# Causal masks as two triangles of 64 columns in a hybrid attention and FFN kernel, with a new order of the work

## The reference

```
x = x + attn_a(layernorm(x))     # 16 heads of 8, RoPE, causal over 256 tokens, softmax, Wo
x = x + ffn(layernorm(x))        # FP4 quantise-dequantise of x, w and h in blocks of 16; silu(gate) * up; down
x = x + attn_b(layernorm(x))     # 16 heads, causal within windows of 32 tokens, RMS norm on q and k
x = x + ffn(layernorm(x))        # the same weights again
```

## Time and profile before

| | |
|---|---|
| median of 3 runs | 422.82 us (422.71 to 425.64) |
| the profiled execution, its own time | 420.45 us |
| its span, first to last instruction | 418.6 us |
| PE matmul busy | 327.8 us (78%), 3533 instructions |
| DVE busy | 293.8 us (70%), 746 instructions |
| ACT busy | 242.2 us (58%), 630 instructions |
| POOL busy | 150.2 us (36%), 210 instructions |

### The profile page before, as it was taken

One profiled execution on the slowest core, in us unless ns is written; L12 is line 12 of the kernel. 1 busy time (PEld: TensorE's weight loads), 2 busy tenths in 40 slices (PEclk: granted clock), 3 DMA queues, 4 the chain that ended last, 5 costly groups with the idle time before them and its releaser, 6 DMA issues.

```text
span 418.6 us, 9181 instructions
## 1 busy us (share of the span) xinstructions
PE 327.8 (78%) x3533; PEld 220.8 (53%) x3533; DVE 293.8 (70%) x746; ACT 242.2 (58%) x630; POOL 150.2 (36%) x210
## 2 busy tenths in 40 slices
PE   1416689778989997999999989997898676665844
PEld 1314446445666754767676666665457445453523
DVE  2835323839677889699987989788747867847741
ACT  2300064226578485488689789787669475592421
POOL 6230042213362037181572251603822553523323
PEclk9999968869899989999999999999699799998565
DMA  6252026605125025020451000000000000000000
GB/s 176 80 113 37 4 76 118 134 3 128 26 81 89 5 63 89 4 78 2 79 128 27 2 4 2 3 16 14 2 2 14 2 0 14 2 14 1 13 14 13
DMA packets 33103, 17.49 MB, mean 42 GB/s; under 512 B 1874, under 2 KB 32914, under 8 KB 33060
## 3 DMA queue, kind: packets, MB, share of 16 engines
q1 hardware_dynamic: 32772, 16.78, 18.3%
q10 hardware_dynamic: 288, 0.13, 0.1%
HBM read 9.37 MB, written 7.34 MB: 40 GB/s over the span
## 4 chain that ended last, share of the span: by engine, by line
PE 39%; DVE 25%; ACT 15%; issue 12%; POOL 4%; DMA 3%; SPq 2%; DVEq 0%; POOLq 0%; ACTq 0%
DVE bmax L1360 6%; PE fb L881 5%; PE fb L799 4%; PE ffb L997 4%; PE fb L869 3%; PE fb L838 3%; ACT prob L1083 2%; PE ffb L975 2%; PE lb L938 2%; PE ffb L991 2%; PE fb L888 2%; PE fb L871 2%; ACT Kd L1126 1%; PE fb L840 1%; PE ffb L979 1%
## 5 line engine op out<-in xcount | busy, mean ns | idle before, releaser
L1360 DVE TENSOR_REDUCE bmax<-fb 128x3 f32<-128x384 f32 x128 | 66.8, 549 | 20.7 <-PE fb L841 19.7
L1083 ACT ACTIVATE prob<-fb 128x384 f32<-128x384 f32 x128 | 59.3, 496 | 24.0 <-PE fb L872 23.3
L838 PE MATMUL fb<-Kf,Qf 48*128 48x256 bf16 x128 | 32.2, 300 | 13.3 <-DMA Kf<-scr_f 7.3
L869 PE MATMUL fb<-Qf,Kf 51*128 51x256 bf16 x128 | 31.3, 295 | 5.2 <-ACT prob L1083 4.4
L840 PE MATMUL fb<-maskb 64*128 64x256 bf16 x128 | 32.3, 300 | 0.0
L1222 POOL TENSOR_TENSOR qk<-ra,rb 128x512 f32<-128x512 f32 x7 | 8.9, 1272 | 63.9 <-DVE rb L1341 63.9
L871 PE MATMUL fb<-maskb 64*128 64x256 bf16 x128 | 31.1, 292 | 0.0
L881 PE MATMUL fb<-prob,Vf 128*32 128x128 f32 (+1 forms) x512 | 29.9, 354 | 1.4 <-ACT prob L1083 1.2
L838 PEld LDWEIGHTS fb<-Kf,Qf 48*128 48x128 bf16 x128 | 10.6, 94 | 31.3 <-DVE bmax L1360 17.5
L839 PE MATMUL fb<-Kf,Qf 48*128 48x128 bf16 x128 | 25.5, 234 | 0.0
L841 PE MATMUL fb<-maskb 64*128 64x128 bf16 x128 | 25.3, 232 | 0.0
(11 more groups left out here) (201 smaller groups left out, 962.7 us busy)
## 6 DMA issues: line engine op xcount, KB each, us to landing
scr_f<-partsf SPq DMA_DIRECT2D x16, 192.0 KB, 2.3
Qf<-scr_f SPq DMA_DIRECT2D x16, 192.0 KB, 3.6
Kf<-scr_f SPq DMA_DIRECT2D x16, 192.0 KB, 5.0
scr_f<-partsf SPq DMA_DIRECT2D x16, 128.0 KB, 1.9
xall<-in_L_attn_a_x_dram SPq DMA_DIRECT2D x8, 128.0 KB, 4.9
scr_f<-partsf SPq DMA_DIRECT2D x16, 64.0 KB, 1.6
out_dram<-xall SPq DMA_DIRECT2D x8, 128.0 KB, 1.8
ropet<-in_rope_dram SPq DMA_DIRECT2D x1, 512.0 KB, 4.1
```

Of the source, the lines that this page charges most:

```text
L838: pe.matmul(S[:, 128:384], Qf[k, g, 128:256], Kf[k, g, 0:256], start=True, stop=True, skip_group_check=True)
L869: pe.matmul(S[:, 128:384], Kf[k, g, 0:128], Qf[k, g, 0:256], start=True, stop=True, skip_group_check=True)
L1083: act.activation(prob[:, slot % 8, :], S[:, 0:384], ACT.Exp).then_inc(f.s_exp, 1)
L1360: dve.tensor_reduce(bmax[:, h, 1:4], fb[:, h % 2, 0:384].rearrange("p (n k) -> p n k", k=P), AX.X, ALU.max).then_inc(bmax_done, 1)
```

## The change

The causal mask of a diagonal tile of 128 x 128 has four quarters of 64 x 64: a triangle, nothing, a triangle, and one wholly masked quarter (first half of the queries, second half of the keys). Before, the first mask matmul wrote a triangle and the constant quarter together, 128 columns for each tile. Now it writes the triangle only, 64 columns. The constant quarter comes out of the score matmuls: two more rows in the stacks, `Qf` one where the token is in quarter 0 (in the other row, quarter 2), `Kf` -1e30 where the token is in quarter 1 (quarter 3). `front2` score matmuls read 50 rows, `front3` ones 53. At the start six more DMAs load the rows of `Qf`, and the six of `Kf` carry five rows instead of three. The mask constants have 128 columns fewer.

The order of all engines is written anew, and so is `FFN_TURNS`. The words that came with the change also name maxima subtracted by DVE; the diff has no such edit, and `local2` does so before and after.

```diff
 NSTACK = HD * NC
-KROWS = NSTACK + 3
+MROWS = NSTACK + 2
+KROWS = MROWS + 3
...
-    full = np.full((64, 64), NEG)
-    halves = np.concatenate([eye[0:64], eye[64:128], lower, full, full, upper], 1)
+    halves = np.concatenate([eye[0:64], eye[64:128], lower, upper], 1)
+    tok = np.arange(SEQ)
+    q_rows = [tok // 64 == 0, tok // 64 == 2]
+    k_rows = [np.where(tok // 64 == 1, NEG, 0.0), np.where(tok // 64 == 3, NEG, 0.0)] + 3 * [np.ones(SEQ)]
...
-        "ones": bf16_bits(np.ones((3, PAIRS * SEQ))),
+        "ones": bf16_bits(np.tile(np.stack(q_rows + k_rows), (1, PAIRS))),
...
             for i in range(RING):
                 for r in range(2):
-                    sp.dma_start(Kfs[i][64 * r + NSTACK:64 * r + KROWS, :, :].rearrange("p g t -> p (g t)"), ones.bitcast(BF16)).then_inc(k_loaded, 16)
+                    sp.dma_start(Kfs[i][64 * r + NSTACK:64 * r + KROWS, :, :].rearrange("p g t -> p (g t)"), ones.bitcast(BF16)[2:7, :]).then_inc(k_loaded, 16)
+                    sp.dma_start(Qfs[i][64 * r + NSTACK:64 * r + MROWS, :, :].rearrange("p g t -> p (g t)"), ones.bitcast(BF16)[0:2, :]).then_inc(k_loaded, 16)
...
-                    row = 64 * r + NSTACK
+                    row = 64 * r + MROWS
...
-                            pe.wait_ge(k_loaded, 16 * (1 + 2 * RING))
+                            pe.wait_ge(k_loaded, 16 * (1 + 4 * RING))
...
-                    k = slice(64 * r, 64 * r + NSTACK)
+                    k = slice(64 * r, 64 * r + MROWS)
...
-                    pe.matmul(ends(S, 0, 128), eye_lo[half_, :], twice(m_qk[half_, :]), start=False, stop=True, skip_group_check=True)
-                    mm = pe.matmul(ends(S, 64, 64), eye_hi[half_, :], twice(m_qk[half_, 0:64]), start=False, stop=True, skip_group_check=True)
+                    pe.matmul(ends(S, 0, 64), eye_lo[half_, :], twice(m_qk[half_, :]), start=False, stop=True, skip_group_check=True)
+                    mm = pe.matmul(ends(S, 64, 64), eye_hi[half_, :], twice(m_qk[half_, :]), start=False, stop=True, skip_group_check=True)
...
-                        pe.matmul(two(S[:, 0:256], 0, 128), eye_hi[half_, :], twice(m_kq[half_, :]), start=False, stop=True, skip_group_check=True)
-                        mm = pe.matmul(two(S[:, 0:256], 0, 64), eye_lo[half_, :], twice(m_kq[half_, 64:128]), start=False, stop=True, skip_group_check=True)
+                        pe.matmul(two(S[:, 0:256], 64, 64), eye_hi[half_, :], twice(m_kq[half_, :]), start=False, stop=True, skip_group_check=True)
+                        mm = pe.matmul(two(S[:, 0:256], 0, 64), eye_lo[half_, :], twice(m_kq[half_, :]), start=False, stop=True, skip_group_check=True)
```

More of the change, by code:

```diff
@@ L63 @@
     "sp.front1": """
-0 1
-8 9
+5 9
 11 12
-15 16
+13 15
+16 17
 19 20
-22 23
-25 27
+23 24
+25 26
 28 29""",
     "sp.front2": """
-7
+10
 14
-17
+18
 21
-24
-26
+22
+27
 30
@@ new lines @@
+445 447 448 450 452 453 456 458 459 461 462 465 466 470 471 475 476 478 479 481 483 489 492""",
+    "pe.local1": """
+123 135 158
+191 196 212
+255 259 267
+321 324 334
+384 389 405
+455 457 468
+497 500 508
+530 531 534""",
+    "pe.local2": """
+163 167 171 175 181 184
+221 222 232 233 236 241
+272 277 294 296 304 305
+343 346 357 362 373 376
+414 420 431 432 439 443
+474 477 485 486 491 494
+512 513 518 519 521 524
+538 539 544 545 546 547""",
+    "pe.ffn_a2": """
+71 74 83 88 92
+128 139 144 149 153
@@ new lines @@
+199 203 204 209 211
+256 260 262 265 266
+316 320 323 325 328
+392 396 399 401 402
+460 463 464 467 469
+505 506 507 509 510""",
+    "pe.ffn_b2": """
+218 223 224 234 237
+271 285 289 299 306
+375 377 378 382 383
+442 446 449 451 454
+493 495 496 498 499
+511 514 515 516 517
+532 533 535 536 537
+552 553 554 555 556""",
+    "pe.ffn_a3": """
+114 116 117 118
+173 174 176 178
+239 240 242 244
+307 309 310 312
+364 365 367 370
+434 435 438 440
+484 487 488 490
+520 522 523 525""",
+    "pe.ffn_b3": """
@@ L181 @@
+333 338 339 350
+409 412 425 429
+472 473 480 482
+501 502 503 504
+526 527 528 529
+540 541 542 543
+548 549 550 551
 557 558 559 560""",
     "act.weights": """
[L183 removed]
+4 5""",
     "act.front1": """
[L185 to L192 removed]
+0 1 2 3
+7 10 13 16
+24 29 32 34
+39 48 49 53
+72 79 82 83
+107 116 117 123
+169 190 193 200
+214 224 225 228""",
     "act.front2": """
[L194 to L202 removed]
[7 rows of a table removed]
@@ new lines @@
+74 78 87 91 94 100
+121 125 130 136 137 141
+172 176 180 183 184 188
+219 223 227 231 233 237
+262 265 268 274 277 283
+314 317 322 329 330 334
+355 357 361 365 367 371
+386 387 388 390 392 394""",
+    "act.local2": """
+109 110 115
+146 151 158
+202 203 207
+243 247 257
+290 295 304
+341 346 352
+376 377 380
+396 399 401""",
+    "act.ffn_a1": """
+36 38
+71 73
+118 126
+163 170
+208 213
+260 264
+310 316
+356 360""",
+    "act.ffn_a2": """
+42 45 56
+86 89 96
+131 135 138
+177 181 187
+218 222 229
@@ L263 @@
+271 275 279
+325 328 333
+366 368 370""",
+    "act.ffn_b1": """
+129 134
+166 173
+212 215
+269 280
+313 321
+359 364
+382 385
+403 405""",
+    "act.ffn_b2": """
+143 147 156
+195 201 206
+258 259 263
+306 308 320
+353 354 358
+372 375 378
 391 393 395
-403 405 407""",
+407 408 409""",
     "act.ffn_a3": """
-54 67 68
-118 142 144
-149 175 176
-198 211 212
-237 252 253
-300 322 323
-337 345 346 351
-371 372 373 374""",
-    "act.ffn_b3": """
-179 196 197
-259 295 297
-307 341 343
-348 369 370
@@ L279 @@
-377 387 388
-394 400 401
-404 406 408 409
+65 68 70
+103 111 112
+145 159 160
+192 209 211
+240 253 254
+286 300 301
+337 338 348 349
+373 374 379 381""",
+    "act.ffn_b3": """
+162 235 241
+255 289 292
+303 342 345
+351 362 363
+369 383 384
+389 397 398
+400 402 404 406
 410 411 412 413""",
@@ L289 @@
 11 14 15 16
-17 22 23 26
-27 28 29 33
-34 39 41 44
-45 51 52 53""",
+17 23 24 25
+26 30 32 34
+35 47 49 51
+54 60 61 64""",
     "pool.local1": """
-20 24
-38 43
-48 58
-60 65
-67 72
-83 84
-90 94
-101 105""",
+21 27
+31 38
+43 48
+59 62
+68 73
+78 84
+89 95
+104 106""",
     "pool.ffn_a1": """
 12 13
-21 25
-30 31
-40 47
-56 59
-68 69
-77 82
-89 92""",
-    "pool.ffn_b1": """
-32 37
-57 61
-64 66
-73 74
-75 79
-93 95
-104 106
-109 110""",
+20 22
+33 36
+42 45
+55 58
+69 71
+79 82
+91 94""",
+    "pool.ffn_b1": """
@@ L321 @@
+37 39
+44 46
+57 66
+72 74
+80 83
+93 96
+103 105
+112 114""",
     "pool.ffn_a3": """
 18 19
-35 36
-42 46
-54 55
-62 63
-76 78
+28 29
+40 41
+50 53
+63 65
+75 76
 85 86 87 88
-97 98 99 100""",
+99 100 101 102""",
     "pool.ffn_b3": """
-49 50
-70 71
-80 81
-91 96
-102 103
+52 56
+67 70
+77 81
+90 92
+97 98
 107 108
-111 112 113 114
+109 110 111 113
 115 116 117 118""",
     "dve.weights": """
-3 4 5 6 9 10""",
+4 6 7 9 13 15""",
     "dve.front1": """
-0 1 2 7 8 11 12
-13 14 15 37
+0 1 2 3 5 8 10
```

260 lines of the change are left out of this document (82 added, 178 removed), and 110 rows, old and new, of tables (FFN_TURNS, TIMES).

## The result

| | before | changed |
|---|---|---|
| median of 4 runs, taken in turns | 422.76 us (418.78 to 425.64) | 408.02 us (406.49 to 410.12) |
| ratio, 95% interval | | 0.9685 (0.960 to 0.977) |
| profiled execution, its own time | 420.45 us | 406.49 us |
| its span | 418.6 us | 404.6 us |
| PE matmul busy | 327.8 us | 315.1 us |

The kernel became 3.2% faster, where 414.8 us (1.9%) was forecast. So ratios can differ by some tenths of a per cent from a quotient of medians. A second series of runs of the changed kernel gave 0.973 (0.970 to 0.976).

What follows compares the result with a forecast made beforehand. The prediction took PE, 91% busy in the middle, as the bound, DVE next. From a 418.6 us span, masks -6, start -2 and rest of the order 0 gave 410.6, or 414.8 us as median of runs; range 407.5 to 421.5.

Steps and rivals of the forecast that it cites:

- The masks, -6 us: Mask matmuls of front2 and front3, 128 columns fewer 256 times: 6 us less, nearer the chain's 5.5 than the ceiling.
- PE's queue is full there, and a matmul taken from it is time given back: Middle, 60 to 290 us: PE 91% busy, longest wait 3.9 us, so removed matmuls save time until DVE is next limit.
- The ceiling of 12 us: Middle: the most the shorter masks can give, 240 mask matmuls at 0.05 us of PE each.
- the share of L840 and L871 in the chain: First mask matmuls, 2% and 1% of the chain that ended last: 12.6 us, half of it removed, 6.3 us.
- the gain goes into the next limit: Rival, chance 0.15: DVE and ACT's exponentials set front2 and front3; the masks give 1.5 us, 419.3 us in all.
- The start, -2 us: Start's new order: RoPE ahead of FFN weights, head 2 1.2 us earlier, shorter front2(0) pairs 0.75 us; together 2 us.
- a gap ahead of the third: Sign at the start, in front2(0): a 2 us gap ahead of the third bmax, where PE's weights transposes stand.
- The rest of the order, 0 us: New order of middle and end: work moved ahead delays front3(7) and is missing in the end; taken as 0 us.
- The bound of -3: Lower bound on the new order of middle and end: at best 3 us less, with +4 as the other bound.
- whose 91 us hardly shrink, being one batch's latency: End, from batch 7's front residual to its last add: 91 us, held to be one batch's latency that hardly shrinks.
- The clock: Rival, chance 0.04: fewer columns get PE a lower granted clock in the middle; with 0.87 the time is 433 us.
- a last L1397 near 317 us: Sign: the last front residual's last row lies near 317 us, the end 91 us behind; beyond 322 us is wrong.

Runs made afterwards that it cites:

- order_only: The kernel before with its old masks and the changed kernel's new order on every engine; ratio 0.9715 to the kernel before.
- masks_only: The kernel before's order on every engine, with the new masks, stack rows and start DMAs; ratio 1.003 to the kernel before.
- start_and_masks: New masks, rows and DMAs, with the new order up to 60 us and the old order after; ratio 0.994 to the kernel before.
- start_only: Old masks and DMAs, with the new order up to 60 us and the old order after; ratio 0.986 to the kernel before.
- end_only: Old masks, with the old order up to 325 us and the new order from there; ratio 0.998 to the kernel before.
- rest_of_order: Old masks, with the old order up to 60 us and the new order for the rest; ratio 0.984 to the kernel before.
- no_triangles: The changed kernel with both triangle mask matmuls of each head left out in front2 and front3; ratio 0.972 to the kernel before.

## Why the prediction was right, and where it was not

The time lies in the range and on the side that had most of the chance. The sum came out at -8 us where the profiled span moved by -14 (by -11 in the repeat), and two of its three terms were mis-sized in opposite directions: the 6 us that it gives to the masks came from the order. That the total still lies in the range is luck, and the side was right because the start and the rest of the order were worth more than they were priced at.

*The masks, -6 us: measured 0 in the time of the whole kernel.* The difference between the change and order_only is within half a per cent of nothing (0.9685 and 0.973 against 0.9715; the intervals allow some 2 us either way), masks_only is at 1.003, and start_and_masks is no better than start_only. The step that failed is "PE's queue is full there, and a matmul taken from it is time given back". It rested on 91% of busy time and on 3.9 us of shown waits. The 3.9 us are the longest group only; all shown waits of PE there add up to 18 us. Both views are blind to pauses under 0.16 us, and columns stream in 74% of the stretch. The ceiling of 12 us was wrong too, since it counted matmuls one after the other of which many run side by side: 7 us by the table. The rest of the costing held: L846 and L847 start 0.06 us apart, the two more rows are free, DVE's maxima keep their length. The other support, the share of L840 and L871 in the chain, isn't a saving either. The chain passes through those matmuls, but it doesn't tell how soon another chain, by way of DVE or ACT, would have ended, and the runs say that one does so almost at once. Of the rivals, "the gain goes into the next limit" had this mechanism and still left the masks 1.5 us. In profiles the last front residual does start 3.5 to 5.5 us earlier with the new masks (322.6 in order_only, 319.1 and 317.2 in the change), near the 6 us, and the spans are 2.4 and 5.6 us shorter. The times of all runs don't bear that out. One place where such a gain can go is in the table of the experiments, and the prediction didn't ask about it: the length of the end goes with its granted clock. In the new order it is 86.9 to 87.6 us at 0.81 to 0.82, 88.7 at 0.79 and 90 at 0.77; in the old order 94 us at 0.80 to 0.81, 95.2 at 0.78 (end_only) and 96.4 to 96.7 at 0.77. All five executions with 0.77 have the new masks, but the two of the change, which has them too, had 0.82 and 0.79. Whether a shorter front brings the lower clock or it is chance is open.

*The start, -2 us: measured -2.5 to -6.* start_only has -6 (0.986), start_and_masks, which has the masks too, -2.5 (0.994). The links stood in the after trace nearly as forecast: remainder 0.69 us (0.7), first scores at 29.69 (30.5), first `bmax` 30.44 (31.4), a gap ahead of the third of 1.64 (2), pairs 1.36 us apart (1.37), and the six DMAs 1.9 us, hidden behind RoPE. The third part is ready at 20.4 us (21.0), SP reads 2.4 us later (2.1 + 0.6), and head 2 starts 2.66 us behind head 0 (3.0). Together head 2 starts 2.3 us earlier (34.67 to 32.35), not 1.2. Why 2.3 us there become up to 6 at the end is not shown.

*The rest of the order, 0 us: measured -7.* rest_of_order has 0.984. The bound of -3 was too near. What failed is "whose 91 us hardly shrink, being one batch's latency". From the last front residual to the last add they shrink to 84.9 us, and to the end of the span from 94.0 to 87.5, with old masks too (87.6 in order_only, 86.9 in rest_of_order). The end is not one batch's latency. Batch 7's steps share their queues with what batches 5 and 6 have left, and less is left when local and FFN work goes ahead in the middle. That batch 7's scales no longer wait for batch 6's adds isn't the gain by itself, for end_only has that too and gains nothing. The prediction named that effect and set it off against a delay of front3(7). The delay came in front3(6), by 4 us in order_only, and was made up by front3(7). That both the middle and the end of the new order are needed is shown (0.998 with the new end alone, 0.991 without it); how much each carries can't be told from these runs.

*The clock*, 0.04: in the changed kernel the middle has 0.94 against 0.95, nothing worth a term. The end, where its executions differ, was not in this rival.

The check "a last L1397 near 317 us" came true (317.15), as the sum's parts had it, and would have been read as proof of the masks' term. The repeat of the same kernel has 319.1. The other half of that check, the last add 91 us behind it, did not come true (84.9).

## What to carry to other kernels

Before pricing a matmul that is taken away, lay out its columns over the granted clock and see how much of the span they fill; if a quarter is unfilled, PE's busy share says little, and an engine with a lower share can be the one on the path. The quickest test is to leave out much more of the suspected work than the change does: twice the mask columns gave nothing, which settled in one experiment what shares and chains had got wrong. Before a small difference between two traces is explained, compare their granted clocks stage by stage. And split a change that rewrites an order from the edit that came with it, since here the order was the whole gain, part of it in a drain that looked like fixed latency.

## What the runs showed of the hardware that was not expected

A matmul's record in the trace is 0.16 us longer than its columns at full clock (0.22 for 0.055), whatever follows it. With some 2500 matmuls in 230 us this fills most gaps: 91% are shown as busy in the kernel before where 74% are streamed, and from it to no_triangles the view lost 12 us where streaming lost 20. The Trainium skill ("Perfetto Trace Analysis", the note at its head) says that matmul busy time is a bad metric for how close a kernel is to its roofline, the most that the engine can do, because matmuls are pipelined; the trace agrees.

Matmuls of 48 to 64 rows on different halves of the array ran side by side without being asked to, two of 256 columns in 0.12 us, which takes 18 of 79 us off the scores and masks of the kernel before.

The granted clock of one kernel differs between executions: 0.82 and 0.79 in the end of the changed kernel, whose end was 87.5 and 88.7 us long.

Both engines pay when GpSimd's two multiplications meet VectorE's two passes. GpSimd's first keeps its 2.54 us, but its second takes 2.42 us in all five traces with the old start and 2.09 to 2.10 in the eight with the new one. In the kernel before, the first ends at 21.23 us and the VectorE pass beside it at 21.78; the second ends at 23.73 and the pass beside it at 24.28. Each pass ends 0.55 us after the multiplication that it met, and alone it takes 0.69 us: it got little or nothing done beside it.
